# Attention scores in four row groups: S and S^T bursts of a cross-attention and expert kernel rearranged

## The reference

```python
def _L0_xattn_ref(q, latent_kv, Wq, Wkv_expand, Wout):
    qp = q @ Wq.T
    kv = latent_kv @ Wkv_expand.T
    k, v = jnp.split(kv, 2, axis=-1)
    ...
    scores = jnp.einsum('bhqd,bhkd->bhqk', qh, kh) * inv_sqrt_d
    scores = jnp.where(causal, scores, jnp.finfo(scores.dtype).min)
    attn = jax.nn.softmax(scores, axis=-1)
    out = jnp.einsum('bhqk,bhkd->bhqd', attn, vh)
    return out @ Wout.T
...
def _L0_ffn_ref(x, ...):
    ...
    gup = jnp.einsum('th,eho->teo', xf, gate_up_proj)
    gup = gup + SCALING * jnp.einsum('ter,eor->teo', jnp.einsum('th,erh->ter', xf, gup_lora_A), gup_lora_B)
    gates, h = jnp.split(gup, 2, axis=-1)
    h = jax.nn.silu(gates) * h
    out = jnp.einsum('tei,eih->teh', h, down_proj)
    ...
x = x + _L0_xattn_ref(_layernorm(x), ctx_512, ...)
x = x + _L0_ffn_ref(_layernorm(x), ...)
```

## Time and profile before

| | |
|---|---|
| median of 3 runs | 184.65 us (184.36 to 184.70) |
| the profiled execution | 183.83 us |
| its span, first to last instruction | 182.1 us |
| busy: PE, DVE, ACT, POOL | 167.4, 105.7, 80.7, 54.1 us |
| mean granted TensorE clock | 0.977 |

### The profile page before, as it was taken

The page is one execution under the profiler, slowest core; times in us unless marked ns, Lnnn a source line. Parts: engine busy times, 40 slices in busy tenths (PEclk is TensorE's granted clock), DMA queues, the critical chain, the costliest instruction groups (busy, mean ns, idle before and its releaser), DMA issues.

```text
span 182.1 us, 3778 instructions
## 1 busy us (share of the span) xinstructions
PE 167.4 (92%) x1481; PEld 134.9 (74%) x1481; DVE 105.7 (58%) x224; ACT 80.7 (44%) x163; POOL 54.1 (30%) x93
## 2 busy tenths in 40 slices
PE   0699999998899999999999999799999999999972
PEld 0466777686778877777878788588888888888862
DVE  3777675765523665546544874568385549444453
ACT  2362264553045455666676456165346422222230
POOL 4265000531322564545756702435000000000000
PEclk9999999999759999999999999999999999999998
DMA  6999910000000000000000000750000188000003
GB/s 157 281 223 289 260 24 2 5 1 4 0 7 0 0 7 0 5 0 5 2 4 0 0 4 23 258 185 4 2 0 0 30 257 296 1 0 0 4 0 115
DMA packets 13041, 11.18 MB, mean 61 GB/s; under 512 B 6456, under 2 KB 10448, under 8 KB 13024
## 3 DMA queue, kind: packets, MB, share of 16 engines
q1 hardware_dynamic: 9584, 7.14, 14.3%
q0 software_dynamic: 544, 2.10, 4.2%
q10 hardware_dynamic: 2896, 1.70, 3.7%
HBM read 9.79 MB, written 1.08 MB: 60 GB/s over the span
## 4 chain that ended last, share of the span: by engine, by line
PE 87%; DVE 5%; issue 2%; DMA 2%; ACT 1%; POOL 1%; DVEq 0%; ACTq 0%
PE bank L803 38%; PE bank L1095 11%; PE bank L916 10%; PE bank L923 8%; PE bank L1032 4%; PE bank L901 4%; PE bank L981 2%; DMA x_sb<-in_x 2%; PE bank L849 2%; PE bank L832 2%; PE bank L884 1%; PE bank L992 1%; PE bank L1013 1%; PE bank L946 1%; DVE x_sb L655 1%
## 5 line engine op out<-in xcount | busy, mean ns | idle before, releaser
L293 POOL TENSOR_SCALAR_AFFINE_SELECT probsT<-probsT 128x512 f32<-128x512 f32 x32 | 19.8, 638 | 40.8 <-ACT probsT L391 40.8
L594 DVE TENSOR_REDUCE m_sb<-bank 128x4 f32<-128x512 f32 x32 | 20.6, 685 | 17.8 <-PE bank L916 17.8
L391 ACT ACTIVATE probsT<-bank 128x512 f32<-128x512 f32 x32 | 17.9, 590 | 29.0 <-PE bank L923 29.0
L316 ACT ACTIVATE h_hi<-h_f 128x512 fp32r<-128x512 f32 x16 | 10.1, 632 | 36.5 <-PE bank L1095 25.3
L803 PE MATMUL bank<-xT_hi,up_hi 128*128 128x512 f32 x64 | 26.0, 406 | 0.0
L916 PE MATMUL bank<-k_f,q_f 32*128 32x128 f32 x256 | 25.4, 291 | 0.0
L803 PE MATMUL bank<-xT_hi,up_lo 128*128 128x512 f32 x64 | 25.3, 395 | 0.0
L803 PE MATMUL bank<-xT_lo,up_hi 128*128 128x512 f32 x64 | 25.3, 395 | 0.0
L923 PE MATMUL bank<-q_f,k_f 32*128 32x128 f32 x256 | 24.3, 282 | 0.0
L916 PEld LDWEIGHTS bank<-k_f,q_f 32*128 32x128 f32 x256 | 19.2, 193 | 6.6 <-issue 6.6
L677 DVE TENSOR_TENSOR h_lo<-h_f,h_hi 128x512 fp32r<-128x512 f32 x16 | 11.5, 720 | 19.1 <-ACT h_hi L316 19.0
(11 more groups left out here) (137 smaller groups left out, 288.9 us busy)
## 6 DMA issues: line engine op xcount, KB each, us to landing
probsT<-weights SPq DMA_DIRECT2D x16, 256.0 KB, 5.5
x_sb<-in_x SPq DMA_DIRECT2D x4, 256.0 KB, 4.7
up_w<-in_L_ffn_gate_up_proj ACTq DMA_DIRECT2D x1, 1024.0 KB, 11.2
up_w<-in_L_ffn_gate_up_proj POOLq DMA_DIRECT2D x1, 1024.0 KB, 7.5
dn_w<-in_L_ffn_down_proj POOLq DMA_DIRECT2D x1, 1024.0 KB, 9.4
out<-x_sb SPq DMA_DIRECT2D x4, 256.0 KB, 2.5
ctx_sb<-in_ctx ACTq DMA_DIRECT2D x2, 128.0 KB, 5.9
wq_raw<-in_L_xattn_Wq ACTq DMA_DIRECT2D x1, 256.0 KB, 6.4
```

Source lines behind the costliest of these rows:

```text
L293: pool.affine_select(out=ch, in_=ch, compare_op=ALU.is_ge, fill=0.0, base=0, pattern=[[0, 4], [1, P]], channel_multiplier=-1).then_inc(S_( ...
L316: act.activation(out_, in_, ACT.Copy, scale=scale).then_inc(S_(done), 1)
L391: act.activation(probsT[:, b % 2, 4 * c:4 * c + 4, :].rearrange("p h n -> p (h n)"), bank[2 + c % 2][:, :], ACT.Exp).then_inc(S_("exp_done ...
L594: dve.reduce_max(m_sb[:, b % 2, :].rearrange("p (u j t) -> p j u t", u=2, t=2)[:, c], S_BANK(b, c)[:, :].rearrange("p (u t n) -> p u t n", ...
```

## The change

The diff is cut to what changes the work or its order; waits that only follow from another bank are left out where they say nothing more.

```diff
+    T_ORDER = (2, 3, 0, 1)
-    MERGE_BANK = lambda n: 4 + n % 4 if n < HC * E // 2 else (4, 6)[n % 2]
+    MERGE_BANK = lambda n: (4, 6, 7)[n % 3] if n < 6 else (4, 6)[n % 2]
-    HIGHS = (0, 4, 1, 5, 2, 6, 8, 9, 3, 7, 10, 11)
-    HIGHS_AT = ((), (0,), (4, 1), (5,), (2,), (6,), (8, 9), ())
+    HIGHS = (0, 4, 1, 5, 2, 3, 6, 8, 9, 7, 10, 11)
+    HIGHS_AT = ((), (0,), (4, 1), (5,), (2,), (3,), (6,), (8,))
...
-        S_BANK = lambda b, j: bank[j if b == 0 else j % 2]
-        M_BANK = lambda b: bank[6 if b else 5][0:NH, PN:PN + P]
+        S_BANK = lambda b, j: bank[j if b < 2 else j % 2]
+        M_BANK = lambda b: bank[6][0:NH, PN:PN + P]
...
-            def scores(s, t, js):
+            def scores(s, s_js, t, t_js):
...
                 for c in range(NC):
                     if s is not None:
-                        for j in js:
+                        for j in s_js:
                             rows = slice(32 * j, 32 * j + 32)
...
                     if t is not None:
-                        for j in js:
+                        for j in t_js:
...
             def on_T(b):
                 pe.wait_ge(S_("oT_copied"), b + 1)
                 if b == 0:
-                    pe.wait_ge(S_("merged"), 6)
+                    pe.wait_ge(S_("wo_ready"), 1)
...
-            scores(0, None, (0, 1))
             pe.wait_ge(S_("wkv_lo"), 2)
-            scores(0, None, (2, 3))
+            scores(0, (0, 1, 2, 3), None, ())
             q_proj(1)
+            k_proj(1)
             max_T(0)
-            scores(1, None, (0, 1))
-            k_proj(1)
-            v_proj((0,))
+            scores(1, (0, 1, 2, 3), None, ())
+            x_T(2)
+            context_T(2)
+            v_proj(0)
             lora_T(0)
             lora_T(1)
-            x_T(2)
-            context_T(2)
-            scores(1, None, (2, 3))
-            q_proj(2)
             for b in range(NT):
-                scores(b + 2 if b + 2 < NT else None, b, (0, 1))
+                scores(b + 2 if b + 2 < NT else None, (0, 1), b, (2, 3))
...
                 if b == 0:
                     k_proj(2)
-                    v_proj((1,))
+                    q_proj(2)
...
-                scores(b + 2 if b + 2 < NT else None, b, (2, 3))
+                scores(b + 2 if b + 2 < NT else None, (2, 3), b, (0, 1))
...
-                    lora_products(range(4))
+                    lora_products(range(3))
...
-                    lora_products(range(4, 8))
+                    lora_products(range(3, 6))
...
-                if b in (GT + 1, GT + 2):
+                if b > GT:
                     pe.wait_ge(S_("oT_copied"), b)
...
-                    lora_products(range(2 * b - 2, 2 * b))
+                    lora_products(range(2 * b - 4, 2 * b - 2))
...
             up_step(2)
+            gate_step(3)
             for n in range(NG * E):
                 if n + 3 < NG * E:
-                    gate_step(n + 3)
                     up_step(n + 3)
+                if n + 4 < NG * E:
+                    gate_step(n + 4)
```

## The result

| | before | after |
|---|---|---|
| median | 184.50 us (183.20 to 184.70, 4 executions) | 171.49 us (170.58 to 172.57, 4 executions) |
| the profiled execution, its span | 183.83, 182.1 us | 170.58, 168.8 us |
| mean granted clock there | 0.977 | 0.998 |

The ratio is 0.931, with a 95% interval of 0.924 to 0.938: faster by 13.0 us. Predicted were 170.0 us, 167.3 to 174.5. The total is close, but it hides a term that failed by 3.6 us.

A forecast was written before the change was run, and what follows sets the result against it. TensorE was taken as the bound, with 87% of the chain of waits. Savings of 2.8 ahead of the loop, 7.8 and 4.7 in stages 0 to 5, less 0.65, sum to 14.6: 184.65 to 170.0 us, range 167.3 to 174.5.

The forecast's parts named there:

- Four row groups: Score bursts: S and S^T in different row groups cut a burst from 2.51 to 1.73 us, 0.78 less.
- Rival 1: Score bursts: feeding takes 0.037 us a record, 0.60 saved in each of 14 bursts; 172.5 us, chance 0.15.
- rival 4: Score bursts: a row group's load waits for the others', pitch stays 0.056 us; 181 us, chance 0.07.
- Ahead of the loop: Before the batch loop: two four-group bursts of 2.24 us replace four of 1.61; stage 0 starts 2.8 us earlier.
- Stages 0 to 5: Batch loop: 7.8 us saved in stages 0 to 2 and 4.7 us in stages 3 to 5.
- the new waits: Stages 0 to 2: about 0.7 us lost to new waits, as where a causal matmul waits for DVE's maxima.
- Rival 3: Stages 1 to 5: DVE becomes the bound, half of ten bursts' gain given back; 174 us, chance 0.08.
- The clock: Stage 2: with on_T(0)'s 1.57 us merge wait gone, the clock doesn't fall to half; 3.4 us saved.
- rivals 2 and 5: Clock falls again in stages 0 to 2, 173.4 us, chance 0.14; clock half through the loop, about 230, 0.04.
- Stages 6 and 7: Lora products 10 and 11 move into stage 7, 0.96 us; a 0.30 us merge wait goes; net -0.65 us.
- The expert loop: Gate one step further ahead fills 1.34 us before the first down step, gate(5) gives 1.1 back; counted 0.
- a few hundredths of margin: Later expert loop: silu ends at 152.97, PE reaches its gate step at 153.00; costs 0 to 0.08 us.

The follow-up runs named there:

- e4: The changed kernel with S and S^T of a burst in the same two row groups again, chunks in order 0 to 3: 180.80 us, ratio 0.986.
- e1: The changed kernel with the expert loop of before, gate three steps ahead: 167.21 us, ratio 0.912.
- e3: The changed kernel with only gate(3) and gate(4) run early, from there on three ahead: 165.96 us, ratio 0.901.
- e2: The changed kernel with ACT's silu(n + 2) issued ahead of its high part of h(n + 1), gate still four ahead: 166.04 us, ratio 0.904.

## Why the prediction was right, and where it wasn't

**Four row groups: right, and better than taken.** The burst came to 1.63 us where 1.73 was predicted: eight quartets in 0.89 us, the ideal of the working, not the 1.00 that the feeding of 0.031 us a record gave. Rival 1 (three groups' worth) and rival 4 (no overlap) fell with the earlier trace rows's counterpart and with e4. The Trainium skill (TensorE: Matmul & The Clock Gate, Measured speedup vs the span model) gives 3.07x for four row tiles, measured with 512 columns where these matmuls have 128. The estimate by it was 0.62 us saved a burst; measured are 0.88, so at 128 columns the trace doesn't agree with it: from two groups to four the pitch of a quartet halved.

**Ahead of the loop: right.** 3.25 instead of 2.8 us; the S burst took 2.05 instead of 2.24, which is 0.4 for two. The 0.6 us up to the first burst differs so between executions and is luck.

**Stages 0 to 5: right in sum.** 8.2 and 4.75 us against 7.8 and 4.7. The bursts gave 0.10 us each more than predicted, 1.2 for twelve, and only 0.45 of it came through: the new waits, foreseen at about 0.7, come to 1.3. Rival 3 (DVE becomes the bound) shows only in the three waits of causal matmuls, 1.1 us of these by their pitches; k_proj(2) to q_proj(2) (26.11 to 26.96) loses another 0.2.

**The clock: right in what came, too sure in why.** It stayed at full level, as predicted, and rivals 2 and 5 didn't come. But "With the wait gone and none above 0.5 us in its place I expect no fall" treated the wait as the whole cause. What the clock gave is also no fixed 3.4 us: before itself ran twice without the fall, in 182.16 and 181.25 us, against medians of 183.8 and 184.2 beside them.

**Stages 6 and 7: too dear by 0.65.** The step that failed is the 0.96 us for the two products, "on the path". PE's timeline of stage 7, before and after:

```profile
97.83 1.16 PE L923 MATMUL bank<-q_f,k_f 32*128 32x128 f32 x16
...
99.18 1.13 PE L803 MATMUL bank<-woT,o_T 128*128 128x256 f32 x4
```

```profile
80.61 0.82 PE L915 MATMUL bank<-q_f,k_f 32*128 32x128 f32 x10
81.25 0.48 PE L798 MATMUL bank<-loraBT,dnA 16*128 16x256 f32 x2
81.27 0.50 PE L915 MATMUL bank<-q_f,k_f 32*128 32x128 f32 x6
...
82.31 1.13 PE L798 MATMUL bank<-woT,o_T 128*128 128x256 f32 x4
```

The products stand behind an S^T burst in two groups and run in other row groups than its tail, as at the seam in the earlier trace rows. From the burst to out_proj it is 82.31 - 80.61 = 1.70 us with them and was 99.18 - 97.83 = 1.35 without, so they cost 0.35 us and not 0.96. The merge's wait that goes gives 0.37 us by its pitch, and the two cancel. I had read that seam for the bursts and not applied it here.

**The expert loop: wrong, the term that failed.** I counted it at 0, with bounds of +0.3 and -1.0, and it is -3.6. The failed step is "a few hundredths of margin, so 0 to 0.08 us over 12 steps". By the rows: PE waits for silu 0.98 us (the one that I foresaw as 1.1), 0.16, 1.29 and 0.57, together 3.0 in brackets. By the pitches from the matmul ahead (1.37, 0.56, 1.69 and 0.97 us, where 0.23 is usual) these four lose 3.7. In the other 7 of the 11 steps in which the weight load waited for silu nothing is idle, and the pitch ahead is longer by 0.03 to 0.05 us, 0.2 in all. Behind each of the 11 the pitch is 0.33 or 0.34, which is 1.1 more. Taken together 5.0; the 1.4 us of the gate step that is done ahead comes off, and 3.6 is what was measured. What I overlooked is in ACT's order: silu stands behind h_hi, and the router's exponential puts a table load of 1.28 us between. At the first and the last of the four waits h_hi itself came late, for h_f on DVE had waited for its transfer of weights. I looked at one later step and took it for all twelve. With e1 to e3 this is shown, not argued: each of three edits removes the waits, and the two that also fill the hole (e2, e3) come to 4.5 and 4.8 us by the spans, where the rows give 5.0.

The forecast of 170.0 us thus came within 1.5 us partly by luck: gains of 2.1 us beyond the plan (0.6 + 0.45 + 0.4 + 0.65), of which the 0.6 has nothing to do with the change, partly hid a loss of 3.6. With the expert loop as it was the kernel takes 167.2, and with the hole filled and no wait for silu 166.

## What to carry to other kernels

Matmuls of 32 rows were worth spreading over all four row groups here, and two kinds of product that are issued together can share the array if each gets its own pair; the gain may be read from the pitch of a quartet. A producer that is moved one step further ahead reuses a bank one step earlier, so look at who must have read that bank, what stands ahead of the reader on its engine, and look at every step of the loop, the irregular ones (table loads, a second chain) first. Fill a hole once instead of deepening a pipeline for good.

## What the runs showed of the hardware that I had not expected

- Four row groups run in a row at twice the rate of two: 32 records of 128 columns go in eight quartets of 0.11 us, 0.028 us a record, against 0.22 and 0.056 with two groups. With filling and draining the score part of a burst is 52.90 - 51.80 = 1.10 us.
- A weight load that waits for a semaphore just in time costs 0.13 to 0.16 us on PE although no idle time is shown (7 places in after). Where idle time is shown, the pitch loses 0.17 us more than the bracket says.
- Small matmuls in row groups that a burst leaves free run beside its tail: two lora products of 0.96 us cost 0.35 there.
- The activation table load takes 1.28 us (124.54 to 125.82), with ACT's next instruction 20 ns behind. The Trainium skill (ScalarE: Activation LUTs, What ACT_TABLE_LOAD costs) gives the same for the load and about as much again for a drain; the load agrees, the drain isn't seen here, where ACT has 20 ns between h_hi and the load.
- Whether the granted clock falls to half behind a pause of TensorE differs between executions of one program: 1 of 4, 3 of 4 and 24 of 26 executions in three kernels, with pauses of 2.38, 1.78 and 1.57 us in their profiled executions.
